# A graph layer with sort, mixing and routed experts on one core: the row loads behind the edge loads, the bias product on VectorE, the front and the gated tiles one sort level sooner, the key store ahead of the last gated rows

## The reference

```python
xn = layernorm(x)                                   # per row, no weights
neigh = xn[dst]                                     # row = src, col = dst
w = sigmoid(relu(neigh @ W1 + b1) @ W2 + b2)        # a gate: depends on the node alone
gnn = segment_sum(neigh * w, src) / segment_sum(w, src)
k, v = headnorm(xn) * wk + bk, headnorm(xn) * wv + bv          # 8 heads of 32
kv = einsum('hnd,hne->hde', k, v) / N
x = x + gnn + (einsum('hnd,hde->hne', xn, kv) + xn)
h = layernorm(x)
top2 of softmax(relu(h @ r1 + rb1) @ r2 + rb2)      # 6 experts, 2 per token
x = x + sum over the 2 of share * expert(h)         # three 256x256 layers each
```

## Time and profile before

| | us |
|---|---|
| median of three runs | 1849.69 |
| the profiled execution's own time | 1852.44 |
| its span | 1850.3 |
| TensorE busy (share of the span) | 1487.4 (80%) |
| VectorE busy | 1346.5 (73%) |
| ScalarE busy | 820.7 (44%) |
| GpSimd busy | 750.7 (41%) |
| mean granted TensorE clock | 0.915 of full |

### The profile page before, as it was taken

One profiled execution on the slowest core, in us unless ns is written; L12 is line 12 of the kernel. 1 busy time (PEld: TensorE's weight loads), 2 busy tenths in 40 slices (PEclk: granted clock), 3 DMA queues, 4 the chain that ended last, 5 costly groups with the idle time before them and its releaser, 6 DMA issues.

```text
span 1850.3 us, 40316 instructions
## 1 busy us (share of the span) xinstructions
PE 1487.4 (80%) x12157; PEld 1373.1 (74%) x12157; DVE 1346.5 (73%) x3891; ACT 820.7 (44%) x1979; POOL 750.7 (41%) x727
## 2 busy tenths in 40 slices
PE   0327776755659999999999999999999659999897
PEld 0226665644549988888888989888888649998786
DVE  6966999989937777777777777776777546676555
ACT  1114343424635555454544454544545325554443
POOL 1497677774431222222212122222213143337776
PEclk9958787856779999999999999999999869999999
DMA  7000000002334110110101010110101055543442
GB/s 173 12 0 1 1 1 1 1 3 78 129 100 142 37 43 35 37 43 31 46 31 48 31 43 34 43 37 32 45 31 48 35 168 138 138 117 96 121 124 77
DMA packets 68021, 108.67 MB, mean 59 GB/s; under 512 B 14164, under 2 KB 47707, under 8 KB 67705
## 3 DMA queue, kind: packets, MB, share of 16 engines
q1 hardware_dynamic: 49720, 56.19, 11.1%
q0 software_dynamic: 18240, 51.74, 7.9%
HBM read 52.41 MB, written 57.47 MB: 59 GB/s over the span
## 4 chain that ended last, share of the span: by engine, by line
PE 59%; issue 15%; POOL 9%; DVE 8%; ACT 3%; DMA 3%; SPq 1%; DVEq 1%; another core or an unknown queue 0%; POOLq 0%; ACTq 0%
PE turned L1386 17%; PE front L1386 15%; PE turned L1368 9%; POOL acc_mem L766 5%; DVE sort_mem L1674 4%; PE turned L1522 4%; PE front L1522 4%; PE front L1542 4%; ACT a_ring L1124 2%; POOL tab_mem L752 2%; DMA gath_mem<-in_dst 1%; PE front L1415 1%; PE turned L1515 1%; PE front L1420 1%; DVE sort_mem L1682 1%
## 5 line engine op out<-in xcount | busy, mean ns | idle before, releaser
L1780 DVE TENSOR_TENSOR sort_mem<-lane_bf,sort_mem 128x512 bf16<-128x512 bf16 x1372 | 500.3, 406 | 204.8 <-PE turned L1368 190.2
L1124 ACT ACTIVATE a_ring<-turned 128x512 fp32r<-128x512 f32 (+2 forms) x686 | 368.8, 544 | 442.1 <-PE turned L1368 437.4
L1386 PE MATMUL turned<-y_all,a_ring 128*128 128x258 f32 x2450 | 388.9, 296 | 30.6 <-ACT a_ring L1124 30.6
L1386 PE MATMUL front<-y_all,a_ring 128*128 128x258 f32 x2352 | 378.9, 298 | 13.0 <-ACT a_ring L1124 11.8
L1386 PEld LDWEIGHTS turned<-y_all,a_ring 128*128 128x128 f32 x2450 | 317.6, 190 | 36.4 <-ACT a_ring L1124 33.7
L1674 DVE TENSOR_TENSOR sort_mem<-sort_mem 128x320 f32<-128x320 f32 (+2 forms) x568 | 326.8, 637 | 3.0
L1386 PEld LDWEIGHTS front<-y_all,a_ring 128*128 128x128 f32 x2352 | 305.9, 189 | 27.7 <-ACT a_ring L1124 23.7
L1368 PE MATMUL turned<-sort_mem 128*128 128x128 bf16 (+1 forms) x2695 | 258.9, 217 | 2.7 <-DVE sort_mem L1780 2.5
L851 POOL COPY feat_mem<-node_id 128x1 int32 (+1 forms) x49 | 9.0, 183 | 445.7 <-DVE list_at L1889 445.7
L1368 PEld LDWEIGHTS turned<-sort_mem 128*128 128x128 bf16 x2695 | 147.8, 98 | 36.6 <-DVE sort_mem L1780 3.6
L2070 DVE COPY acc_mem<-feat_mem 128x1796 f32 x112 | 122.7, 1098 | 24.8 <-issue 24.8
(11 more groups left out here) (256 smaller groups left out, 2293.5 us busy)
## 6 DMA issues: line engine op xcount, KB each, us to landing
base<-token_lists SPq DMA_DIRECT2D x54, 258.0 KB
base<-token_lists SPq DMA_DIRECT2D x54, 130.0 KB
gated_rows<-tab_mem SPq DMA_DIRECT2D x49, 128.5 KB, 2.9
late_mem<-mixed_rows SPq DMA_DIRECT2D x49, 128.0 KB
mixed_rows<-base SPq DMA_DIRECT2D x12, 512.0 KB, 3.5
feat_mem<-in_L_ffn_expert_w SPq DMA_DIRECT2D x18, 256.0 KB, 6.1
base<-in_x SPq DMA_DIRECT2D x1, 3136.0 KB
base<-in_x SPq DMA_DIRECT2D x1, 2352.0 KB
```

The source lines that it names most:

```text
L1124: nc.scalar.activation(a_ring[:, k % 2, :, :].rearrange("p s n -> p (s n)")[:, 0:width], ps_a[k % 2][:, 0:width], ACT.Copy).then_inc(S["a_ ...
L1386: last = nc.tensor.matmul(ps_agg[odd], a_ring[:, k % 2, n, :], y_part(t, part), start=(t == 0 and part == 0), stop=(t == BLOCKS - 1 and pa ...
L1780: nc.vector.tensor_tensor(hot[:, k % 2, 0:pairs, 0:lanes, :], lane_bf[:, 0:lanes, :].unsqueeze(1).broadcast_to([P, pairs, lanes, 2]), edge ...
```

## The change

- SyncE waits for both edge loads before it issues the first part of the rows, then issues the eight small weight loads, then the second part of the rows.
- GpSimd's L752 and L754 go. VectorE makes -mean/std in one `scalar_tensor_tensor` a part, behind the second half of passes (3, 0) and (4, 1), and waits there for GpSimd's power.
- `FRONT_FIRST` has one round more, each later table gives its rounds one number higher, and the last round and `finish_front` follow turn (16, 15) and no longer turn (16, 6).
- Gating and mixing begin behind turn (16, 6). All 49 tiles are gated, and batches up to 10 mixed, ahead of the sort's end; five tiles and one batch came behind it before.
- SyncE stores the sorted keys ahead of the gated rows of tiles 45 to 48, and the row of ones first of all.

```diff
-FRONT_FIRST = (1, 5)
-FRONT_AT = {(8, 6): (5, 7), ... (15, 14): (20, 22)}
-FRONT_END = ((15, 6), (16, 15), (16, 6))
-GATED_AT = {(17, 16): (0, 10), (17, 6): (10, 16), (18, 17): (16, 33), (18, 6): (33, 44)}
-GATED_LAST = 44
-MIX_AT = {(17, 16): (0, 2), (17, 6): (2, 3), (18, 17): (3, 7), (18, 6): (7, 10)}
+BIAS_AFTER = ((3, 0), (4, 1))
+FRONT_FIRST = (1, 6)
+FRONT_AT = {(8, 6): (6, 8), ... (15, 14): (21, 22)}
+FRONT_END = ((15, 14), (15, 6), (16, 15))
+GATED_AT = {(16, 6): (0, 6), (17, 16): (6, 18), (17, 6): (18, 26), (18, 17): (26, 43), (18, 6): (43, BLOCKS)}
+MIX_AT = {(16, 6): (0, 1), (17, 16): (1, 4), (17, 6): (4, 6), (18, 17): (6, 10), (18, 6): (10, 11)}
+KEPT_AFTER = 44
...
+            sp.wait_ge(S["edges_loaded"], 32)
             load_rows(0, at, to)
-            sp.wait_ge(S["x_zeroed"], 1)
-            load_rows(1, rest_at, rest_to)
...
+            sp.wait_ge(S["x_zeroed"], 1)
+            load_rows(1, rest_at, rest_to)
...
             for t in range(FULL):
+                if t == KEPT_AFTER + 1:
+                    for half in range(2):
+                        sp.wait_ge(sorted_half[half], instructions_before(LEVELS, -1, half))
+                    sp.dma_start(kept_chunks, ordered_chunks).then_inc(S["kept_stored"], 16)
                 sp.wait_ge(S["y_ready"], t + 1)
...
-                pool.wait_ge(S["pool_step"], links + 3)
-                nc.gpsimd.tensor_tensor(shift, mean, scale, ALU.mult).then_inc(S["pool_step"], 1)
-                pool.wait_ge(S["pool_step"], links + 4)
-                nc.gpsimd.tensor_scalar(shift, shift, -1.0, None, ALU.mult).then_inc(S["x_norm"], 1)
...
-            for t in range(GATED_LAST, BLOCKS):
-                gated_and_mixed(t, MIX_LAST)
             act.wait_ge(S["kept_stored"], 32)
...
+            def rows_bias(part):
+                at, to = X_PARTS[part]
+                dve.wait_ge(S["pool_step"], ROOTS_READY + 2 * part)
+                nc.vector.scalar_tensor_tensor(x_bias[:, at:to], x_mean_var[:, at:to, 0], -1.0, x_rstd[:, at:to], ALU.mult,
+                                               ALU.mult).then_inc(S["x_norm"], 1)
```

More of the change, by code:

```diff
@@ L57 @@
 STATS_AFTER = ((2, 0), (3, 0))
-FRONT_FIRST = (1, 5)
-FRONT_AT = {(8, 6): (5, 7), (9, 6): (7, 9), (10, 6): (9, 10), (11, 10): (10, 11), (11, 6): (11, 12), (12, 11): (12, 13),
-            (12, 6): (13, 15), (13, 12): (15, 16), (13, 6): (16, 17), (14, 13): (17, 18), (14, 6): (18, 20), (15, 14): (20, 22)}
-FRONT_END = ((15, 6), (16, 15), (16, 6))
-GATED_AT = {(17, 16): (0, 10), (17, 6): (10, 16), (18, 17): (16, 33), (18, 6): (33, 44)}
-GATED_LAST = 44
-MIX_AT = {(17, 16): (0, 2), (17, 6): (2, 3), (18, 17): (3, 7), (18, 6): (7, 10)}
+BIAS_AFTER = ((3, 0), (4, 1))
+ROOTS_READY = 6 + 2 * (P // HEAD_DIM) + 3
+FRONT_FIRST = (1, 6)
+FRONT_AT = {(8, 6): (6, 8), (9, 6): (8, 10), (10, 6): (10, 11), (11, 10): (11, 12), (11, 6): (12, 13), (12, 11): (13, 14),
+            (12, 6): (14, 16), (13, 12): (16, 17), (13, 6): (17, 18), (14, 13): (18, 19), (14, 6): (19, 21), (15, 14): (21, 22)}
+FRONT_END = ((15, 14), (15, 6), (16, 15))
+GATED_AT = {(16, 6): (0, 6), (17, 16): (6, 18), (17, 6): (18, 26), (18, 17): (26, 43), (18, 6): (43, BLOCKS)}
+MIX_AT = {(16, 6): (0, 1), (17, 16): (1, 4), (17, 6): (4, 6), (18, 17): (6, 10), (18, 6): (10, 11)}
 MIX_LAST = 10
+KEPT_AFTER = 44
 MIX_LAG = 5
@@ L596, in store_mixed @@
                 sp.dma_start(mixed_rows[at * P:to * P, :].rearrange("(t p) d -> p t d", p=P), base[:, at:to, :]).then_inc(S["mixed_stored"], 16)
+            sp.wait_ge(S["consts"], N_CONSTS)
+            sp.dma_start(kept_keys[COLS:COLS + 1, :], ones[0:1, :]).then_inc(S["kept_stored"], 16)
             for t in range(FULL):
+                if t == KEPT_AFTER + 1:
+                    for half in range(2):
+                        sp.wait_ge(sorted_half[half], instructions_before(LEVELS, -1, half))
+                    sp.dma_start(kept_chunks, ordered_chunks).then_inc(S["kept_stored"], 16)
                 sp.wait_ge(S["y_ready"], t + 1)
@@ L602, in _ @@
                     store_mixed((t - MIX_LAG) // MIX_TILES)
-            sp.wait_ge(S["consts"], N_CONSTS)
-            sp.dma_start(kept_keys[COLS:COLS + 1, :], ones[0:1, :]).then_inc(S["kept_stored"], 16)
             sp.wait_ge(S["y_ready"], BLOCKS)
             sp.dma_start(y_table[FULL * P:BLOCKS * P, :], y_out[:, 0, 0:ROW]).then_inc(y_stored[0], 16)
-            for half in range(2):
-                sp.wait_ge(sorted_half[half], instructions_before(LEVELS, -1, half))
-            sp.dma_start(kept_chunks, ordered_chunks).then_inc(S["kept_stored"], 16)
             def load_mixed(n, b, slot, count):
@@ L744, in _ @@
             for part, (at, to) in enumerate(X_PARTS):
-                mean, variance, scale, shift = x_mean_var[:, at:to, 0], x_mean_var[:, at:to, 1], x_rstd[:, at:to], x_bias[:, at:to]
-                links = n + 3 * part
+                variance, scale, shift = x_mean_var[:, at:to, 1], x_rstd[:, at:to], x_bias[:, at:to]
+                links = n + 2 * part
                 pool.wait_ge(S["x_stats_ready"], to)
@@ L750, in _ @@
                 nc.gpsimd.tensor_tensor(scale, shift, minus_half[:, at:to], ALU.pow).then_inc(S["pool_step"], 1)
-                pool.wait_ge(S["pool_step"], links + 3)
-                nc.gpsimd.tensor_tensor(shift, mean, scale, ALU.mult).then_inc(S["pool_step"], 1)
-                pool.wait_ge(S["pool_step"], links + 4)
-                nc.gpsimd.tensor_scalar(shift, shift, -1.0, None, ALU.mult).then_inc(S["x_norm"], 1)
-            n += 7
+            n += 5
             def spread(u, tiles, first):
@@ L1447, in pe_alone @@
                     pe_pieces(n, j, slot)
-            mix(MIX_LAST)
             pe.wait_ge(S["lanes_f_ready"], 1)
@@ L1711, in _ @@
                         exchange(*passes[n - LAG], 1)
+                        if passes[n - LAG] in BIAS_AFTER:
+                            rows_bias(BIAS_AFTER.index(passes[n - LAG]))
                         if passes[n - LAG] in STATS_AFTER:
```

## The result

The changed kernel takes 1830.71 us in the median of four runs (1826.64 to 1835.73); the kernel before took 1851.59 beside it, median of four. The ratio is 0.9895, 95% interval 0.9868 to 0.9921: about 21 us faster, where 56 were forecast. The profiled execution took 1826.64 us, its span is 1824.9, the mean granted clock 0.912.

The account below looks back on a forecast made before the run. The chain is 59% TensorE, but the change acts before 535 us, on VectorE's waits. Terms: 14.8 + 24.8 - 0.4 + 4.0 - 1.6 + 14.2 = 55.8 us, from 1849.7 to 1794 us; range 1786 to 1804, 8 in 10 1785 to 1829.

Parts of the forecast that it names:

- term 1: Start: edges loaded ahead of the rows let VectorE begin at 11.4 us, not 26.21; 14.8 us saved.
- term 2: First section: bias product on VectorE, GpSimd's first power L766 admitted, first turn sooner; 24.8 us saved, less 0.4 for products.
- Term 3: End of the front: VectorE's wait of 5.06 us shrinks to about 1; 4 us saved.
- Term 4: Sort: five more splits run beside it, at 0.33 us each; 1.6 us lost.
- term 5: End of the sort: key store issued at about 509.0, not 524.42, gather begins at 514.7; 14.2 us saved.
- rival C: Start: rows come late, at 58 GB/s, second part landing at 122 us; 7.1 us lost, 1857 us; chance 3%.
- Rival B: First section: some of the twenty operations of the first five rounds is held; about 1810 us; chance 18%.
- rival A: First section: the first L766 is held to the section's end like the product it replaces; 1826 us; chance 22%.

Follow-up runs that it names:

- before_third: The unchanged kernel before, profiled a third time, in set E: 1851.20 us, ratio 1.0022 to before.
- set A: Runs sharing one chip: pause_first, a version with pauses in nearly all sections, no_shift and after_again, with the kernel before beside them at 1851.36 us.
- before_again: The unchanged kernel before, run again for a second profile: 1870.28 us, ratio 1.0014 to before.
- loads_alone: The kernel before with only the new order of the loads: 1858.62 us, ratio 0.9948 to before.
- keys_alone: The kernel before with only the new place of the key store in SyncE's program: 1864.27 us, ratio 0.9967 to before.
- two_nops: The kernel before with two do-nothing instructions in VectorE's program where the change has its two products: 1848.06 us, ratio 0.9982 to before.
- after_again: The changed kernel, unaltered, run again for a second profile: 1826.72 us, ratio 0.9894 to before.
- bias_alone: The kernel before with only the bias product moved from GpSimd to VectorE: 1843.35 us, ratio 0.9961 to before.
- no_shift: The changed kernel with the old tables of the front, gating and mixing: 1826.69 us, ratio 0.9874 to before.
- pause_first: The changed kernel with VectorE waiting once a pass for its own last instruction, first section, from the fourth level on: 1802.39 us, ratio 0.9736 to before.

## Why the prediction was wrong, step by step

With before_third both sides have the same aggregation (910.3 and 911.4 us), so the terms are measured between it and after, two profiles of different sets:

| | forecast | from | measured |
|---|---|---|---|
| term 1, loads | 14.8 | 26.41 to 15.38 | 11.0 |
| term 2, product and first turn | 24.4 | 153.20 to 147.72, less term 1 | -5.5 |
| terms 3 and 4, turn to sort's end | 2.4 | 366.4 to 370.0 | -3.6 |
| term 5, sort's end to window | 14.2 | 25.1 to 9.8 | 15.3 |
| sum | 55.8 | 544.72 to 527.54 | 17.2 |

The first two rows repeat within about 1 us from profile to profile of a kernel. The third does not: from the turn to the sort's end the three profiles of before have 355.9, 374.2 and 366.4 us, and the two of the change 370.0 and 372.3, so its -3.6 could as well be -16 or +4. The medians fell by 20.9 us, and by 24.6 in set A.

- **Term 1** named the right mechanism and took its rate from a window in which edges and rows flow together. The edges alone had 122 to 133 GB/s. The rows came in time; rival C fell.
- **Term 2** is the step that failed, by 30 of the 39 us between forecast and sum. The sum has no hold in it for any operation of the first rounds, and the second of them was held for 31.91 us. Its choice, "I take it as admitted", came true for the power. The error is what followed it: "Beside a streaming VectorE a round takes 8.54 us" was used for all operations behind it. Rival B had "about 3% each" for a hold, counted in the later sections, and the count itself doesn't give 3%: six of those 100 operations were held, and of the 75 that directly follow another, one. In the first section the third or fourth operation behind the second statistics was held to the end in all ten profiles without pauses or copies there: the product in before, before_again, before_third, loads_alone, keys_alone and two_nops, the add in after, after_again, bias_alone and no_shift. With the hold lifted (pause_first) the turn comes at 119.13, 34.1 us before before_third's, which is term 1 and 23.0 us more: the size of term 2 was right, had nothing been held. It is rival B, whose price of about 1810 us was for a hold in the middle; it came at the second of the twenty operations, where the price is rival A's, 1826.
- **Term 3**: the wait at the end of the front is 4.13 us, not about 1. **Term 4**: a stretch of twenty took 12.91 us for 11.92. The trace of before has four splits beside that stretch, not "about six", and the one of after has six, so a split costs 0.5 us and not 0.33: 2.5 for the five. Together: from VectorE's first instruction behind the turn to the sort's end it is idle for 31.5 us in after and 34.8 in before_third, 3.3 less where term 3 had 4, but busy for 335.7 and 329.7. Those 6.0 us more stand where term 4 had 1.6; what makes up the rest of them is not shown.
- **Term 5** was right in size (5.71 us from count to window, forecast 5.3 to 6) and so was its account of the splits. no_shift and keys_alone show that the store and the tables only do it together.
- The **baseline**: the profiled execution stood within 2.7 us of the median and was taken as typical. It was not, but its two departures nearly cancel, so this cost the sum little. It did cost the reading of the result: comparing the first two traces alone puts 12 us of the gain into the aggregation.

## What to carry to other kernels

If GpSimd works beside a VectorE stream of instructions with two SBUF inputs, look for the first operation that is stretched to the stream's end, and give the stream openings all along (a wait for its own result, or an instruction with one input) before moving the operation: the next one inherits the hold, and after a single opening the one after that does. Count a hold's chance in the same stretch, not in ones that have openings. And before two traces are compared stage by stage, take a second profile of the old kernel: here two of them are 18.4 us apart at the end of the same sort.

## What was not expected of the hardware

- GpSimd operations that read SBUF were held for 25.9 to 35.0 us beside VectorE's two-input stream. In all eleven such holds of the first section the only gap lies at the end: it is 0.03 us long, and a held add or 28-column product ends less than 0.1 us behind it. A one-column copy with one input, 0.14 us long, did the same with no gap at all. Others were admitted at a mere boundary between two instructions, such as the add of 0.52 us in pause_first. What decides between the two stays open. The Trainium skill (SBUF — State Buffer, Who interferes with whom) gives the shared ports to whoever issues first, for one whole instruction; the 31.91 us here span 68.
- The same kernel spends 909.5 or 926.0 us in the same 49 rounds on two chips, with a granted clock of 1.00 from 560 to 1440 us in both.
- Two loads of 0.8 MB each, with nothing beside them, move at 122 to 133 GB/s; with the row loads beside them the sum is 206.
